# Two attention layers on one core: bias jobs three steps apart, a query load ahead of the fills, and transposes of the maxima behind the next two jobs

## The reference, cut to what matters

```python
# layer 0, on x normalised in 32 groups
rel_h = jnp.einsum('bhwc,hkc->bhwk', r_q, Rh)
rel_w = jnp.einsum('bhwc,wkc->bhwk', r_q, Rw)
attn_bias = (rel_h[:, :, :, :, None] + rel_w[:, :, :, None, :]).reshape(Bx * NUM_HEADS, S, S)
scores = q @ jnp.swapaxes(k, -1, -2) * SCALE + attn_bias
attn = jax.nn.softmax(scores, axis=-1)
out = attn @ v
# layer 1, on its own normalised input
scores = jnp.where(mask_cat[None, None], scores, NEG_INF)
attn = jax.nn.softmax(scores, axis=-1)
```

## Time and profile before

| | us |
|---|---|
| median of 3 runs | 4898.58 (4896.02 to 4903.14) |
| profiled execution | 4902.5 |
| its span in the trace | 4900.8 |
| PE busy | 4491.2 |
| DVE busy | 3079.3 |
| ACT busy | 2608.5 |

### The profile page before, as it was taken

One profiled execution on the slowest core, in us unless ns is written; L12 is line 12 of the kernel. 1 busy time (PEld: TensorE's weight loads), 2 busy tenths in 40 slices (PEclk: granted clock), 3 DMA queues, 4 the chain that ended last, 5 costly groups with the idle time before them and its releaser, 6 DMA issues.

```text
span 4900.8 us, 97559 instructions
## 1 busy us (share of the span) xinstructions
PE 4491.2 (92%) x32598; PEld 2291.5 (47%) x32598; DVE 3079.3 (63%) x5558; ACT 2608.5 (53%) x3955; POOL 892.5 (18%) x1901
## 2 busy tenths in 40 slices
PE   5879999999999999999999999999999999999998
PEld 3334453544535454453544535455454544535444
DVE  3736667665675656667566675656657566676654
ACT  1533556555564555556555564555646555565564
POOL 3112111222202212121212202212021121102111
PEclk7888999999999999999999999999999999999999
DMA  6334242443414433253433424433144432424401
GB/s 126 83 73 86 49 104 62 99 90 70 89 39 106 87 87 71 53 108 70 99 79 70 88 52 99 94 73 84 44 106 81 99 79 48 101 62 99 87 14 40
DMA packets 235869, 386.05 MB, mean 79 GB/s; under 512 B 58396, under 2 KB 133728, under 8 KB 235360
## 3 DMA queue, kind: packets, MB, share of 16 engines
q1 hardware_dynamic: 189280, 266.13, 23.8%
q10 hardware_dynamic: 21504, 75.51, 7.6%
q0 software_dynamic: 24576, 37.80, 4.8%
HBM read 227.79 MB, written 88.08 MB: 64 GB/s over the span
## 4 chain that ended last, share of the span: by engine, by line
PE 75%; DVE 9%; SPq 5%; issue 5%; DMA 5%; ACT 2%; DVEq 0%; ACTq 0%; POOL 0%
PE P L1135 15%; PE P L1153 14%; PE P L1094 13%; PE P L958 6%; PE P L959 6%; DVE mx L901 5%; PE P L1071 5%; PE P L1185 4%; PE P L1206 4%; PE P L1102 3%; DMA QA<-queries 2%; PE P L1178 1%; SPq L507 1%; DMA biases<-xn 1%; DVE mxc L907 1%
## 5 line engine op out<-in xcount | busy, mean ns | idle before, releaser
L901 DVE TENSOR_REDUCE mx<-P 128x1 f32<-128x512 f32 x3072 | 1923.2, 682 | 471.2 <-PE P L1094 467.9
L771 ACT ACTIVATE probs<-P 128x1024 f32<-128x1024 f32 x1536 | 1507.5, 1022 | 777.7 <-PE P L1153 777.0
L1094 PE MATMUL P<-K,AR 96*128 96x256 f16 x6144 | 1093.1, 282 | 42.9 <-DMA AR<-biases 26.7
L1153 PE MATMUL P<-AR,K 113*128 113x512 f16 x3072 | 924.8, 383 | 14.1 <-DMA AR<-mrow 13.6
L907 DVE TENSOR_REDUCE mxc<-P 128x1 f32<-128x336 f32 (+1 forms) x1536 | 648.2, 474 | 307.6 <-PE P L1103 304.0
L787 ACT ACTIVATE probs<-P 128x320 f32<-128x320 f32 (+3 forms) x1632 | 618.1, 436 | 405.2 <-PE P L1206 340.0
L1135 PE MATMUL P<-probs,V 128*17 128x512 f32 x6144 | 817.2, 604 | 9.9 <-ACT probs L771 9.9
L1094 PEld LDWEIGHTS P<-K,AR 96*128 96x128 f16 x6144 | 541.7, 99 | 566.9 <-DVE mx L901 198.3
L1153 PEld LDWEIGHTS P<-AR,K 113*128 113x128 f16 x3072 | 216.9, 98 | 676.6 <-ACT probs L771 517.8
L1206 PE MATMUL P<-A,K 113*128 113x320 f16 (+2 forms) x1536 | 447.1, 306 | 12.9 <-ACT probs L787 12.1
L1102 PE MATMUL P<-K,A 112*128 112x320 f16 (+1 forms) x1536 | 400.4, 295 | 53.4 <-DVE mx L901 35.8
(11 more groups left out here) (122 smaller groups left out, 3705.4 us busy)
## 6 DMA issues: line engine op xcount, KB each, us to landing
AR<-biases SPq DMA_DIRECT2D x384, 256.0 KB, 7.7
AR<-queries ACTq DMA_DIRECT2D x96, 512.0 KB, 5.8
biases<-xn SPq DMA_DIRECT2D x192, 256.0 KB, 2.9
AR<-queries ACTq DMA_DIRECT2D x96, 256.0 KB, 8.5
K<-oraw POOLq DMA_DIRECT2D x384, 64.0 KB, 4.8
xin<-in_x_dram SPq DMA_DIRECT2D x16, 768.0 KB, 10.5
queries<-oraw SPq DMA_DIRECT2D x384, 32.0 KB, 4.8
QA<-queries SPq DMA_DIRECT2D x192, 64.0 KB, 5.1
```

Source lines behind the costliest of these rows:

```text
L771: nc.scalar.activation(probs[:, u % RING, j:j + 2, :], P[:, b:b + 2, :], ACT.Exp).then_inc(p_done[0], 1)
L901: V_.reduce_max(mx[:, n // 2, n % 2:n % 2 + 1], bank, AX.X).then_inc(used, 1)
L1094: last = mm(bank[:, QD * (v % 2):QD * (v % 2) + QD], AR[0:ROWS_MAX[0], part % SLOTS, v, c, j, 128 * q:128 * q + 128], K0[0:ROWS_MAX[0], h, ...
L1153: last = mm(P[:, j, :], K0[0:ROWS, h, 128 * kt:128 * kt + 128], AR[0:ROWS, p % SLOTS, kt // 2, :, j, :], start=True, stop=True)
```

## The change

It has four parts.

1. The four bias jobs of a set stand three steps apart. Set 0: steps 2, 5, 8, 11 (before 2 to 5). Set 1: 17, 20, 23, 26 (before 24 to 27). Set 2: 8, 11, 14, 17 (before 8 to 11). Fill 0 moves from step 5 to 11, ask 1 and fill 1 from 6 to 12.
2. The load of set 1's queries is issued at the end of `operands_out`, ahead of set 0's biases and of the fills.
3. `rows_later` moves each transposition behind the next two jobs (at most two steps). In the global stage those of phases 3, 4 and 5 then stand behind two maximum jobs of what follows, in the local stage that of step 60 behind one; those at steps 93 and 97 have nothing behind them and stay.
4. `mx` is doubled, and the transpositions get semaphores of their own (`row_done`, `row_used`), because the jobs behind them are now read earlier.

```diff
+def rows_later(placed):
+
+    for at in [n for n, (_, job) in enumerate(placed) if is_row(job)][::-1]:
+        to, passed = at, 0
+        while passed < 2 and to + 1 < len(placed):
+            follower = placed[to + 1][1]
+            if placed[to + 1][0] > placed[at][0] + 2 or is_row(follower) or follower[1] == 1 and placed[at][1][1] == 1 and follower[0] == "max":
+                break
+            to, passed = to + 1, passed + (follower[0] not in MOVES)
+        row = placed.pop(at)
+        placed.insert(to, (placed[to - 1][0] if to > at else row[0], row[1]))
+    return placed
...
-    placed += [(8 + n, job) for n, job in enumerate(rel_jobs(image, 2))]
+    placed += [(8 + 3 * n, job) for n, job in enumerate(rel_jobs(image, 2))]
...
-    placed += [(2 + n, job) for n, job in enumerate(rel_jobs(n0, 0))]
-    placed += [(0, ask(n0, 0)), (5, fill(n0, 0)), (6, ask(n0, 1)), (6, fill(n0, 1))]
-    placed += [(24 + n, job) for n, job in enumerate(rel_jobs(n0, 1))]
+    placed += [(2 + 3 * n, job) for n, job in enumerate(rel_jobs(n0, 0))]
+    placed += [(0, ask(n0, 0)), (11, fill(n0, 0)), (12, ask(n0, 1)), (12, fill(n0, 1))]
+    placed += [(17 + 3 * n, job) for n, job in enumerate(rel_jobs(n0, 1))]
...
-        mx = sb("mx", [128, ITEMS[0] // 2, 2])
+        mx = sb("mx", [128, 2, ITEMS[0] // 2, 2])
...
+                query_blocks(im, 1)
...
-                    if part in (0, 2):
-                        query_blocks(image, part // 2 + 1)
+                    if part == 2:
+                        query_blocks(image, 2)
```

More of the change, by code:

```diff
@@ L114, in evenly, with is_row @@
     return placed
+def is_row(job):
+    return job[0] == "max" and job[4] == ITEMS[job[1]]
+def rows_later(placed):
[9 more added lines that the diff above has]
+    return placed
 def plan(steps, placed):
     after, jobs = [[] for _ in range(steps)], []
-    for place, job in sorted(placed, key=lambda p: p[0]):
+    for place, job in rows_later(sorted(placed, key=lambda p: p[0])):
         if job[0] in MOVES:
@@ L316, in attention_kernel @@
         mid_out, mid_in = sem("mid_out"), sem("mid_in")
-        smax_done = sems("smax_done")
-        smax_used = sems("smax_used")
+        smax_done, row_done = sems("smax_done"), sems("row_done")
+        smax_used, row_used = sems("smax_used"), sems("row_used")
         comb_done = sem("comb_done")
@@ L333, in attention_kernel @@
         out_in = sem("out_in")
-        PER_ITEMS = [PHASES[n] * (ITEMS[n] + 1) for n in range(2)]
+        PER_ITEMS = [PHASES[n] * ITEMS[n] for n in range(2)]
         PER_Q, PER_K, PER_QA, PER_AR = 12 * 16, 12 * 16, 4 * 16, 6 * 16
@@ L382, in consumed @@
                 return stat_used[layer], image * 2 + n + 1
-            return smax_used[layer], image * PER_ITEMS[layer] + part * (ITEMS[layer] + 1) + n + 1
+            if is_row(job):
+                return row_used[layer], image * PHASES[layer] + part + 1
+            return smax_used[layer], image * PER_ITEMS[layer] + part * ITEMS[layer] + n + 1
         def rel_view(bank, n, operand):
@@ L893, in low_parts @@
                     if what == "max":
-                        dve.wait_ge(smax_done[layer], value)
+                        dve.wait_ge((row_done if is_row(job) else smax_done)[layer], value)
                         if n == ITEMS[layer]:
@@ L900, in low_parts @@
                         elif layer == 0:
-                            V_.reduce_max(mx[:, n // 2, n % 2:n % 2 + 1], bank, AX.X).then_inc(used, 1)
+                            V_.reduce_max(mx[:, part % 2, n // 2, n % 2:n % 2 + 1], bank, AX.X).then_inc(used, 1)
                             if n == ITEMS[0] - 1:
                                 dve.wait_ge(used, value)
-                                V_.tensor_reduce(mxc[0][:], mx[:], AX.X, ALU.max).then_inc(comb_done, 1)
+                                V_.tensor_reduce(mxc[0][:], mx[:, part % 2, :, :], AX.X, ALU.max).then_inc(comb_done, 1)
                         else:
@@ L1103, in run_job @@
                     last = mm(bank[:, cols:cols + REG], lhs, K1[0:ROWS_MAX[1], h, S:S + REG], start=True, stop=True)
-                last.then_inc(smax_done[layer], 1)
+                last.then_inc((row_done if is_row(job) else smax_done)[layer], 1)
             def run_jobs(entries, L):
```

## The result

The changed kernel takes **4954.1 us** (median of four runs, 4944.2 to 4958.1), where the kernel before took 4900.4 beside it. The ratio is 1.0115, 95% interval 1.0096 to 1.0134: slower by 54 us, and 28 us above the upper end of the range. The profiled execution has a span of 4954.7 us against 4900.8.

The account below looks back on a forecast made before the run. PE, busy 92% of the span, bounds the kernel through in-order waits and half clock. Terms 14 - 21 - 8 + 8 - 2.5 = -9.5 us on 4900.8 give 4891.3; the runs' median lies 2.2 lower: 4889 us, range 4856 to 4926.

Parts of the forecast that it names:

- The landing of set 0's writes: Local stage: set 0's four bias writes, with ask 1 close by, take 9.2 us to land instead of 5.0.
- The sign named for it: Profile after, local stage: a bias job's wait for `biases` of 4 to 8 us, 14 times.
- PE at the bias job: Local stage, step 17: PE reaches set 1's first bias job at about 2395.4, then idles 6.0 us for the landing.
- From the restart to step 30: Local stage, from the landing at 2401.4 to step 30's scores: 4.2 + 1.8 + 0.8 + 11.8 - 4.0 us.
- the term of 4.0 us: Local stage, set 1: saving of up to 4.0 us, since the clock returns some 5 us behind the restart.
- rival B: Local stage: clock stays low through set 1, 3.5 us lost a turn instead of 1.0; 4924 us, chance 0.20.
- The load "costs nothing": Local stage: loading `QA` costs nothing, issued 7 us earlier; it delays SP by 1.8 us, but SP waits anyway.
- Set 2 in the global stage: Global stage, 16 times: spreading set 2's bias jobs saves 1.3 us a stage, 21 us; bounds 0 and 2.7.
- Transpositions in the local stage: Local stage: the 0.69 us wait goes, as one maximum job stands ahead; minus 0.6 us a turn, 8 us.
- Transpositions in the global stage: Global stage, phases 3 to 5: later rows of maxima hold up scores; plus 0.5 us a stage, 8 us.
- Before the loop: Ahead of the loop: two transpositions with 1.5 us of idleness get other jobs ahead of them; minus 2.5 us.
- C: Rival: global stage gives nothing; ring waits only move, rows of maxima come late in all three phases; 4918 us, chance 0.13.

Follow-up runs that it names:

- experiment 4: Changed kernel with ask 1 and fill 1 in step 20 of the local stage instead of 12: 4894.2 us, ratio 0.9992.
- experiment 7: Changed kernel without `rows_later`, transpositions back behind the last maximum job of their row, doubled `mx` and semaphores kept: 4921.1 us, ratio 1.0038.
- experiment 2: Kernel before with only set 2's bias jobs three steps apart (8, 11, 14, 17): 4882.9 us, ratio 0.9961.
- experiment 3: Kernel before with only the transpositions moved later, with doubled `mx` and the new semaphores: 4961.9 us, ratio 1.0127.
- experiment 8: Changed kernel with ask 1 and fill 1 at local step 20 and the transpositions put back in the global stage alone: 4865.9 us, ratio 0.9936.
- experiment 5: Changed kernel with the places of ask 5 and fill 5 in the global stage three steps later: 4922.1 us, ratio 1.0040.
- the last pair: Kernel before with load behind set 0's writes, set 2 apart, ask 1 at step 16, local transpositions later: 4823.8 us; with set 1 apart too: 4828.5.

## Why the prediction was wrong

- **The landing of set 0's writes.** Right. It said start 15.1 us into the stage, 9.2 us to land, landing at 24.3; it was 15.4, 8.9, 24.3. The sign named for it (a wait of 4 to 8 us, 14 times) came at or just under the lower end: 14 waits of 3.6 to 5.3 us.
- **PE at the bias job.** Mis-sized, without harm. Forecast 18.3 us into the stage, measured 20.5 in the case shown and 20.1 on average. The registers' product did get the full clock (1.96 us). But the two column jobs, though three steps apart, still ended in a low stretch, 14.3 us into the stage in the case shown. The step "I expect no low clock there any more" failed in nine turns of 14 and held in five, in four of which PE came at 18.9. Either way PE then stood until the landing, so this error cost nothing at step 30.
- **From the restart to step 30.** This is the step in the local stage that failed: the term of 4.0 us, taken off because the clock was to come back, is too large. The clock did come back, some 3.6 us behind the restart (the forecast said 5), and in ten turns was lost again in set 1 (low at 2445.5 in the case shown). From the landing to step 30 were 16.4 us instead of 14.6. The second low stretch explains only 0.5 of that, since the four turns without it took 15.9. And in experiment 4, where PE has the same instructions there, three turns with the full clock all the way took 14.3 to 14.5 us from set 1's first job to step 30. So the 14.6 of the sum, meant to hold 5 us of low clock, was what no low clock at all gives. The part cost 1.9 us a turn at step 30 (40.65 against 38.71) instead of 1.0, and 1.4 at step 101 with the transpositions' gain in it; experiment 7's trace, without that gain, has 28 us for the local stages in place of the forecast's 14. By the sign that the prediction named (a low stretch over 10 us) rival B holds in the turns like the one shown, with 13.6 us, and not in the five with 6.8. Its price of 3.5 us a turn didn't come in either.
- **What the sum never asked.** It priced the collision against the kernel before, found it nearly free, and went on. Without the collision the same places bring step 30 4.6 us earlier (experiment 4). The term was not 1.0 because the new wait is cheap, but because a large gain and a large loss cancelled. A sum that holds an avoidable 9.2 us landing should have been set beside the 5.0 of the earlier trace rows.
- **The load "costs nothing".** True in the changed kernel, where set 0's writes come late anyway: in the stage shown the load's issues end at 2420.88, 1.9 us ahead of the first write. For the load itself it is not true: alone it costs 43 us. I looked at when SP's next issue was due, not at what the load waits for.
- **Set 2 in the global stage.** Right in sign; in size only by experiment 2's medians (20 us for 21, interval 12 to 26). In the changed kernel the steps 20 to 44 run 1.1 us ahead, but turns with no low clock up to there are only 0.5 ahead (37.8 us against 38.2 at step 20). The rest is that three of its 14 turns have a low stretch there and nine of the kernel before, a count that changes from run to run (7 in experiment 2's trace, 4 in experiment 3's, which leaves set 2 alone). Over the 14 global stages the traces of experiments 2, 7 and 8, with set 2 apart and no transposition moved there, are 7 to 10 us ahead, 0.5 to 0.7 a stage where the sum took 1.3. So this term may have been twice too large; no run settles it.
- **Transpositions in the local stage.** Right: 0.6 us at step 60 (steps 60 to 64 in 2.26 us instead of 2.84).
- **Transpositions in the global stage.** This failed most. Forecast plus 8, bounds minus 8 and plus 16 (minus 0.5 and plus 1.0 a stage); the traces of the changed kernel and of experiment 7 give plus 38. Less the 7 won in the local stages that is 31 of the 33 between their medians. Two things were missed. First, the rows are late without any collision, by some 1.1 us a stage (0.5 in phase 3, 0.5 in phase 4, 0.1 in phase 5, in experiment 5's trace), where the sum has 0.5; phase 4, taken as a gain of 0.1, was a loss. Secondly, and this is the larger part, the landing of a row was taken as the page's median, 1.7 us, and the queue of ACT was not looked at. The move brought the rows of phase 3 within 0.3 us of ask 5. The trace of before could have told: ask 5 stands 1.36 us behind the last row there, and the sum itself makes the row 1.3 us later. Moving the ask away took 32 us back (experiment 5).
- **Before the loop.** Forecast minus 2.5; it was plus 3.7 up to the first stage and plus 12.1 in the first block. The second goes wholly with ask 5 late (experiment 5), so it is the same collision. The 3.7 stay unexplained. The changed kernel without the moved transpositions has 3.9 there (experiment 7), so nothing of the forecast's gain shows; and the other variants have minus 0.3 to 3.6, 1.7 even in experiment 2, which changes nothing ahead of the first stage, so part of it isn't the change's.
- **The rivals.** C came nearest: it let the rows come late in all three phases, for 8 us more, and took set 2's gain away. The rows alone cost 38 instead of its 16. None of the four had a row of maxima that meets an ask, and none went beyond 4924.

## What to carry to other kernels

When a step is moved on one queue, look at where every other queue's large transfers stand then, above all for small transfers whose landing something waits for: a median landing time holds only for the old neighbours. A distance that was enough can shrink by a move that looks unrelated: here 1.36 us was enough and 0.26 was not. Ask of a DMA that is issued earlier not only what it delays by its issue but what its own wait holds up in the queue; the best place is where the queue waits anyway. And where a sum contains a cost that the change brings upon itself, price the change without it as well: here moving one ask, with its fill, by eight steps was worth 60 us.

## What the runs showed of the hardware

- A transfer of 768 KB on ACT's queue, issued 0.35 us ahead, raised the landing of each 256 KB write on SP's queue from 2.5 us (experiment 4) to 6.8 us, at the same place in the same stage.
- A 4 KB row issued 0.26 us ahead of a 768 KB ask on another queue landed in 1.7 us in eight turns and in 3.8 to 6.3 us in six, at the same distance. Being first in time did not protect it. A distance of 1.36 us (the kernel before, all 16 global stages) did, as did 5.4 us (experiment 5, all 16). A fill of 1 MB on the row's own queue, 0.7 us behind it, did no harm there (experiment 5).
- The column jobs take 2.04 to 2.08 us at either clock level, where the row jobs take 0.63 at the full level and 1.01 to 1.06 at half. Three steps apart they still stood ahead of low stretches in nine of 14 turns; spreading set 1's made the low time of a local stage shorter (9.2 to 7.4 us in the last pair) without making the stage shorter.
